# Identity products beside the waits of TensorE in a two-layer decoder kernel

## The chip, the cores and the metric

The kernel runs as one program on one core of a Trainium2 chip. The metric is the device time of one execution in microseconds (us), the median of several runs; lower is better.

## The reference, cut to what matters

```python
x = x + _L0_attn_ref(_layernorm(x), ...)                     # state-space scan, 8 x 512 x 256
x = x + _L0_xattn_ref(_layernorm(x), ctx_1024, ctx_1024, ...) # attention, 16 heads of 16, 1024 keys
x = x + _L0_ffn_ref(_layernorm(x), ...)                      # three quantised blocks with LoRA
x = x + _L1_attn_ref(_layernorm(x), ...)                     # self-attention, 16 heads of 16, 512 keys
x = x + _L1_xattn_ref(ctx_1024, _layernorm(x), ...)          # latent attention, 16 heads of 64, 1536 keys
x = x + _L1_ffn_ref(_layernorm(x), ...)                      # ternary weights, integer activations
...
attn = jax.nn.softmax(jnp.einsum('bhqd,bhkd->bhqk', q, k) * SCALE, axis=-1)
out = jnp.einsum('bhqk,bhkd->bhqd', attn, v)
```

The softmax of each attention is computed against the exact maximum of each row, so the kernel computes the scores twice: once for the maxima, and once more, shifted, for the exponentials.

## The kernel before

`build` runs one `phase` after another: constants, ssm_inputs, scan, ssm_outputs, attention_inputs (tiles `ci_`), attention (`ca_`, 1024 keys), lora_ffn (`ff_`), attention_inputs (`ai_`), attention (`aa_`, 512 keys), latent_inputs (`li_`), latent_attention (`la_`) and ternary_ffn (`tf_`). Each phase ends with a barrier of all engines (L3317), so that no engine begins the next before all have finished.

`attention` walks 32 units (8 sequences x 4 groups of 4 heads). A unit has KT key tiles, 8 in `ca` and 4 in `aa`; "a key tile" below is one turn of the loop `for kt in range(KT)`. In it TensorE issues, in this order written by hand, the scores of four heads (L1765, one 512-column product each, into three banks of PSUM that `ScalarE` must have emptied), the products of exponentials and values of the key tile before (`weigh`, L1774, eight records), and between them a part of the work of the next unit: the maximum pairs (`max_pair`, L1758). A pair is two products of 48 rows side by side in the array, and VectorE reduces its 1024 columns to row maxima (L1898). The two pair banks make a pair wait until the pair two before it is reduced. When the last pair of a unit is reduced, VectorE negates and transposes the maxima, and a DMA (`shift_row`, L1701) writes them as an extra row of the queries; the unit's scores wait for it (`shift_done`).

Before unit 0 there is an opening: 19 pairs in `ca` (`MP + FIRST`, MP = 16) and 11 in `aa` (MP = 8), then two products that make the bias (L1808), and then the wait for the shift row. Unit 0's key tiles carry further pairs to catch up (`CATCH_UP`): in `ca` 3, 3, 3, 2, 2 and so on, in `aa` 2, 3, 3, 3. The last pair of all belongs to unit 31. Behind it come key tiles without a pair: in `ca` the last three of unit 30 and the eight of unit 31, 11 in all; in `aa` the last two and the four, 6 in all. Then a tail: `turn`, `turn_back` and five `project` (L1798), each with a copy or sum on another engine.

`latent_inputs` ends with value projections and stores; SyncE must load `lw_nT` back before the barrier opens. `latent_attention` begins with three projections, 12 maximum pairs (`max_pair`, L2705), four transposes of the negated maxima (`shifts`, L2713), two copies by ScalarE (L2847), and then its units' scores (L2722, L2723). `ternary_ffn` begins with a normalisation on VectorE, GpSimd and ScalarE, after which TensorE turns the tokens (L3075).

Of the kernel before, what the change touches and what calls it, by code (L numbers as in the profile page):

```python
# [13 lines left out]
P = 128  # L14
B, T, D = 8, 512, 256
TC = 1024
NT = T // P
KD = D // P
# [45 lines left out]
def sems(nc, ctx, tag, names):  # L64

    made = [nc.alloc_semaphore(f"{tag}_{n}") for n in names.split()]
    ctx.extend(made)
    return made


class NormBuffers:
# [1533 lines left out]
def attention(nc, io, g, semctx, tag, keys, loads, bo, bv, beside=None):  # L1605
# [8 lines left out]
    MP = GH // 2 * NT * HALVES  # L1614
    assert MP == 2 * KT
    UNITS = B * GROUPS
# [2 lines left out]

    AHEAD, FIRST = 6, 3  # L1620
    OUT, TURN, BACK = 0, 2, 3
    PAIRS = {8: (2, 2, 2, 2, 2, 2, 2, 2), 4: (1, 3, 1, 3)}[KT]
    CATCH_UP = {8: (1, 1, 1, 0, 0, 0, 0, 0), 4: (1, 0, 2, 0)}[KT]
    assert sum(PAIRS) == MP and sum(CATCH_UP) == AHEAD - FIRST
# [47 lines left out]
    with ExitStack() as ctx:  # L1672
# [31 lines left out]
        with nc.Block() as block:  # L1704
# [21 lines left out]
            def _(pe):  # L1726
# [74 lines left out]

                for j in range(MP + FIRST):
                    max_pair(j)
                pe.wait_ge(w_loaded, 16)
                pe.wait_ge(bias_step, KD)
                out = max_banks("bias", 0)
                for k in range(KD):
                    last = pe.matmul(out[:, 0, 0:D], bv_wide[:, k, :], w_o[:, k, :], start=(k == 0), stop=(k == KD - 1))  # L1808
                last.then_inc(bias_step, 1)
                pe.wait_ge(ones_loaded, 32)  # L1810
                for unit in range(UNITS):
                    u = unit % GROUPS
                    pe.wait_ge(shift_done, 64 * (unit + 1))
                    for kt in range(KT):
                        early, late, behind = pairs_of(unit, kt)
                        scores(unit, u, kt, 0)
                        scores(unit, u, kt, 1)
                        for j in early:
                            max_pair(j)
                        for kind, n in after(unit, kt):  # L1820
                            if kind == "turn":
                                turn(n)
                            elif kind == "back":
                                turn_back(n)
                            else:
                                project(n)
                        scores(unit, u, kt, 2)
                        for j in late:
                            max_pair(j)
                        scores(unit, u, kt, 3)  # L1830
                        if kt > 0:
                            weigh(unit, u, kt - 1)
                        elif unit > 0:
                            weigh(unit - 1, (u - 1) % GROUPS, KT - 1)
                        for j in behind:
                            max_pair(j)
                weigh(UNITS - 1, GROUPS - 1, KT - 1)
                turn(UNITS - 1)
                turn_back(UNITS // 2 - 1)
# [602 lines left out]
def latent_inputs(nc, io, g, semctx, weights):  # L2442
# [3 lines left out]
    with ExitStack() as ctx:  # L2446
# [13 lines left out]
        with nc.Block() as block:  # L2460
# [18 lines left out]
            @block.tensor  # L2479
            def _(pe):  # L2480
                pe.wait_ge(xv_loaded, 16)
                for b in range(B):
                    values.project(pe, b, 0, xv)
                    values.project(pe, b, 1, xv)
                    pe.wait_ge(xnorm2.normed, NT * b + NT)

                    if b:
                        pe.wait_ge(nT_done, KD * b)
                    for c in range(KD):
                        for j in range(NT):  # L2490
                            last = pe.transpose(tp[:, c, j * P:(j + 1) * P], xn[:, j, c * P:(c + 1) * P], g.ident[:, :])
                    last.then_inc(lat_ready, 1)
                    values.project(pe, b, 2, xv)
                    values.project(pe, b, 3, xv)

            @block.scalar
            def _(act):
# [41 lines left out]
def latent_attention(nc, io, g, semctx, weights):  # L2539
# [19 lines left out]
    with ExitStack() as ctx:  # L2559
# [57 lines left out]
        with nc.Block() as block:  # L2617
# [45 lines left out]
            def _(pe):  # L2663
# [147 lines left out]
                pe.wait_ge(v_done, 1)  # L2811
                for n in range(NM):
                    max_pair(0, 0, 0, n)
                shifts(0)
                units(unit_steps)
                for x in range(2):
                    for h in range(2):
# [187 lines left out]
def ternary_ffn(nc, io, g, semctx):  # L3005

    KI = INNER // P
    with ExitStack() as ctx:
# [46 lines left out]
        with nc.Block() as block:  # L3055
# [12 lines left out]
            @block.tensor  # L3068
            def _(pe):
                def turn_tokens(b):  # L3070
                    pe.wait_ge(xq_done, b + 1)
                    pe.wait_ge(xT_done, b)
                    for c in range(KD):
                        for j in range(NT):
                            last = pe.transpose(tp[:, c, j * P:(j + 1) * P], xq[:, j, c * P:(c + 1) * P], g.ident_bf[:, :])  # L3075
                    last.then_inc(tp_ready, 1)

                def gate(n):
                    if n % NT == 0:
                        pe.wait_ge(xT_done, n // NT + 1)  # L3080
                    pe.wait_ge(gated_done, n)
                    hidden(n, g_ps, w_gate).then_inc(g_ready, 1)

                def up(n):
                    pe.wait_ge(h_done, n)
                    hidden(n, u_ps, w_up).then_inc(u_ready, 1)

                def hidden(n, ps, w):
                    rows = slice(n % NT * P, n % NT * P + P)
                    for half in range(2):  # L3090
                        for k in range(KD):
                            last = pe.matmul(ps[:, half, :], xqT[:, k, rows], w[:, k, half * T:(half + 1) * T],  # L3092
                                             start=(k == 0), stop=(k == KD - 1))
                    return last

                def turn_hidden(n):
                    pe.wait_ge(hq_done, n + 1)
                    pe.wait_ge(hT_done, n)
                    for k in range(KI):
                        last = pe.transpose(ht_ps[:, k, :], hq[:, n % 2, k * P:(k + 1) * P], g.ident_bf[:, :])  # L3100
                    last.then_inc(ht_ready, 1)

                def down(n):
                    pe.wait_ge(hT_done, n + 1)
                    pe.wait_ge(x_done, n)
                    for k in range(KI):
                        last = pe.matmul(y_ps[:, 0:D], hqT[:, k, :], w_down[:, k, :], start=(k == 0), stop=(k == KI - 1))  # L3107
                    last.then_inc(y_ready, 1)

                turn_tokens(0)  # L3110
                pe.wait_ge(w_loaded[0], 16)
                gate(0)
                pe.wait_ge(w_loaded[1], 16)
                up(0)
                for n in range(TILES + LAG):
                    if n >= LAG:
                        if n == LAG:
                            pe.wait_ge(w_loaded[2], 16)
                        down(n - LAG)
                    if n + 1 < TILES:  # L3120
                        gate(n + 1)
                        up(n + 1)
                    if 0 < n <= TILES:
                        turn_hidden(n - 1)
                    if of(n, INTEGERS) is not None:
                        turn_tokens(of(n, INTEGERS))
# [304 lines left out]
```

## Time and profile before

| | us |
|---|---|
| median of 3 runs | 5219.44 |
| lowest and highest | 5215.84, 5220.12 |
| the profiled execution: its time | 5224.77 |
| its span, first to last instruction | 5222.9 |
| TensorE busy | 4837.2 (93%) |
| VectorE busy | 3661.5 (70%) |
| ScalarE busy | 2929.2 (56%) |
| GpSimd busy | 2638.9 (51%) |
| mean granted TensorE clock | 0.965 |

The granted clock is given as a share of 2.4 GHz: 1.00 is 2.4 GHz and 0.50 is 1.2 GHz. A busy TensorE is not TensorE at its peak, since its matmuls are pipelined and their ends are modelled. Starts are microseconds from the start of the span.

### The profile page before, as it was taken

What the parts mean: (1) busy time and instruction counts of PE and PEld (TensorE: products, weight loads), DVE (VectorE), ACT (ScalarE), POOL (GpSimd) and SP (SyncE); (2) the same over time, 40 slices, a digit from 0 to 9 for tenths busy, and PEclk for the clock granted to TensorE, in tenths of its full rate; (3) what the DMA queues carried; (4) which work ended last, traced back from release to release, by engine and by line L of the source; (5) the groups of instructions that cost most, each with busy time, mean ns of one, the idle gap of its engine ahead of it and who ended that gap; (6) DMA issues with size and microseconds to landing.
All of it is one profiled execution on the core that took longest, in us unless ns stands there. A gap on an engine that the chain in (4) does not pass through costs nothing. (4 is left out here: it accounts for less than half of the span.)

```text
span 5222.9 us, 71135 instructions
## 1 busy us (share of the span) xinstructions
PE 4837.2 (93%) x23995; PEld 2650.3 (51%) x24010; DVE 3661.5 (70%) x6589; ACT 2929.2 (56%) x6224; POOL 2638.9 (51%) x1552
## 2 busy tenths in 40 slices
PE   6899997799999898899879999999999999999976
PEld 5555555344444487444455555555555555555533
DVE  8666666688888588688746666666666766666668
ACT  5677773377777543476534444444444444444557
POOL 5555554200000142521037777777777778787740
PEclk9999998799999799899989999999999999999989
DMA  6566667432222003523363433334333333333300
GB/s 220 192 232 240 230 235 224 132 84 74 72 74 69 12 1 113 178 85 87 114 195 75 100 85 90 91 83 97 80 94 85 89 97 81 94 89 85 89 17 29
DMA packets 344187, 576.29 MB, mean 110 GB/s; under 512 B 49120, under 2 KB 142368, under 8 KB 342800
## 3 DMA queue, kind: packets, MB, share of 16 engines
q1 hardware_dynamic: 341616, 567.53, 37.7%
q8 instruction: 193, 3.16, 0.2%
q10 hardware_dynamic: 2208, 4.20, 0.2%
q14 instruction: 170, 1.39, 0.1%
HBM read 335.54 MB, written 201.85 MB: 103 GB/s over the span
## 5 line engine op out<-in xcount | busy, mean ns | idle before, releaser
L2913 POOL TENSOR_TENSOR la_acc<-la_acc,la_pr 128x1024 f32<-128x1024 f32 x704 | 1697.0, 2411 | 494.5 <-ACT la_pr L2871 459.2
L2871 ACT ACTIVATE la_pr<-la_s_ps 128x512 f32<-128x512 f32 x1536 | 793.7, 603 | 973.2 <-PE la_s_ps L2723 971.5
L2730 PE MATMUL la_o_ps<-la_pr,la_vf 128*64 128x512 f32 x3072 | 743.8, 605 | 0.0
L2722 PE MATMUL la_s_ps<-la_q_hl,la_k_hh 128*128 128x512 f32 x1536 | 691.6, 450 | 1.8 <-ACT la_q_hs L2847 1.4
L1898 DVE TENSOR_REDUCE ca_mx<-ca_m_ps 128x2 f32<-128x1024 f32 x512 | 600.8, 1217 | 118.7 <-PE ca_m_ps L1758 118.5
L1860 ACT ACTIVATE ca_pr<-ca_s_ps 128x512 f32<-128x512 f32 x1024 | 542.1, 601 | 215.6 <-PE ca_s_ps L1765 212.3
L2940 DVE TENSOR_REDUCE la_mx<-la_m_ps 128x2 f32<-128x1024 f32 x384 | 462.9, 1206 | 215.3 <-PE la_m_ps L2705 206.7
L2723 PE MATMUL la_s_ps<-la_q_hs,la_k_l 65*128 65x512 f32 x1536 | 608.8, 396 | 0.0
L2940 DVE TENSOR_REDUCE la_mx<-la_misc 128x2 f32<-128x1024 f32 x384 | 466.1, 1214 | 0.0
L2722 PEld LDWEIGHTS la_s_ps<-la_q_hl,la_k_hh 128*128 128x128 f32 x1536 | 290.0, 189 | 243.4 <-ACT la_pr L2871 103.7
L2730 PEld LDWEIGHTS la_o_ps<-la_pr,la_vf 128*64 128x64 f32 x3072 | 186.3, 136 | 346.8 <-issue 227.3
L1898 DVE TENSOR_REDUCE aa_mx<-aa_m_ps 128x2 f32<-128x1024 f32 x256 | 306.2, 1216 | 66.5 <-PE aa_m_ps L1758 63.3
L1860 ACT ACTIVATE aa_pr<-aa_s_ps 128x512 f32<-128x512 f32 x512 | 275.5, 602 | 118.5 <-PE aa_s_ps L1765 118.3
L1765 PE MATMUL ca_s_ps<-cl_qs,cl_ks 49*128 49x512 f32 x1024 | 330.2, 474 | 8.8 <-ACT ca_pr L1860 5.5
L2723 PEld LDWEIGHTS la_s_ps<-la_q_hs,la_k_l 65*128 65x128 f32 x1536 | 292.3, 190 | 36.1
L2314 POOL MEMSET ff_bias<- 128x768 f32 x1 | 0.7, 737 | 611.7 <-POOLq L3317 611.7
L2952 DVE RECIPROCAL la_rden<-la_den 128x128 f32<-128x128 f32 x256 | 241.3, 944 | 88.4 <-ACT la_den L2857 88.4
L2964 DVE TENSOR_TENSOR g_x<-g_x,la_misc 128x512 f32<-128x512 f32 x128 | 88.0, 688 | 303.5 <-PE la_misc L2749 303.5
L1758 PE MATMUL ca_m_ps<-cl_ks,cl_qs 48*128 48x512 f32 x1024 | 254.8, 493 | 45.6 <-DVE ca_mx L1898 34.7
L1774 PE MATMUL ca_o_ps<-ca_pr,cl_vs 128*32 128x512 f32 x2048 | 283.8, 628 | 0.0
L1765 PEld LDWEIGHTS ca_s_ps<-cl_qs,cl_ks 49*128 49x128 f32 x1024 | 137.5, 193 | 240.0 <-ACT ca_pr L1860 188.7
L916 PE MATMUL sc_jobs<-sc_n_parts,cw_xk 128*128 128x512 f32 x768 | 246.7, 429 | 0.0
(405 smaller groups left out, 8822.8 us busy)
## 6 DMA issues: line engine op xcount, KB each, us to landing
la_k_hh<-scratch_k_high SPq DMA_DIRECT2D x128, 512.0 KB, 6.5
scratch_k_high<-sc_k_high SPq DMA_DIRECT2D x128, 256.0 KB, 2.6
scratch_k_low<-sc_k_low SPq DMA_DIRECT2D x128, 256.0 KB, 2.8
la_w_parts<-scratch_w_parts SPq DMA_DIRECT2D x64, 512.0 KB, 6.2
la_k_l<-scratch_k_low SPq DMA_DIRECT2D x64, 512.0 KB, 8.4
la_vf<-scratch_xv SPq DMA_DIRECT2D x64, 512.0 KB, 4.2
cl_ks<-scratch_k_rows SPq DMA_DIRECT2D x384, 64.0 KB, 2.8
scratch_vaug<-sc_v SPq DMA_DIRECT2D x16, 1024.0 KB, 4.4
```

What stands on the lines that cost most here:

```text
L916: return pe.matmul(jobs[:, bank, :], stationary, moving, start=(i == 0), stop=(i == len(products) - 1))
L1758: last = pe.matmul(out[:, i, :], qs[rows, u, r, qt:T:NT], ks[rows, u, r, half * T:(half + 1) * T], start=True, stop=True)
L1765: pe.matmul(out, ks[rows, u, r, kt * P:(kt + 1) * P], qs[rows, u, r, :], start=True, stop=True).then_inc(s_ready, 1)
L1774: last = pe.matmul(o_ps[32 * h:32 * h + 32, :], vs[:, u, kt, h, :], pr[:, 2 * (kt % 2) + h // 2, h % 2, :], start=(kt == 0), stop=(kt == K ...
L1860: act.activation(pr[:, 2 * (kt % 2) + h // 2, h % 2, :], s_ps[:, s_turns.bank("tile", n), :], ACT.Exp, scale=scale).then_inc(p_done, 1)
L1898: dve.tensor_reduce(mx[:, unit % 2, qt, r:GH:2, half], m_ps[:, m_turns.bank("max", j), :, :], AX.X, ALU.max).then_inc(m_reduced, 1)
L2722: pe.matmul(s_ps[:, bank, :], k_hh[:, par, h, keys], q_hl[:, par, h, :], start=True, stop=False)
L2723: pe.matmul(s_ps[:, bank, :], k_l1[:, par, h, keys], q_hs[:, par, h, :], start=False, stop=True).then_inc(s_ready, 1)
L2730: last = pe.matmul(o_ps[XD * h:XD * h + XD, :], vf[:, par, st, XD * h:XD * h + XD], pr[:, st % LAG, h, :], start=(st == 0), stop=(st == XT ...
L2871: act.activation(pr[:, st % LAG, h, :], s_ps[:, (2 * st + h) % 3, :], ACT.Exp, scale=scale).then_inc(p_done, 1)
L2913: pool.tensor_tensor(total, total, exps, ALU.add).then_inc(acc_done, 1)
L2940: dve.tensor_reduce(mx[:, qt, :, c], pair_banks(i)[:, :, :], AX.X, ALU.max).then_inc(m_reduced, 1)
```

## The change

A helper `keep_busy(pe, g, bank, count)` issues `count` products of the 128 x 128 f32 identity with itself, with no wait and no signal, into a part of a PSUM bank that nothing reads then. It is called:

- in `attention` (both), three products behind each of the opening pairs, 24 behind the bias products, and three at the end of each key tile that has no pair (with a wait that all pairs are reduced);
- at the end of `latent_inputs`, 36 products;
- in `latent_attention`, three behind each of the 12 opening pairs, and 16 behind the transposes of `shifts(0)`;
- at the start of `ternary_ffn`, 48 products ahead of `turn_tokens(0)`.

```diff
+def keep_busy(pe, g, bank, count):
+
+    for _ in range(count):
+        pe.matmul(bank, g.ident[:, :], g.ident[:, :], start=True, stop=True)
...
+    BESIDE_PAIR, BESIDE_SHIFT = 3, 24
...
                 for j in range(MP + FIRST):
                     max_pair(j)
+                    keep_busy(pe, g, o_ps[:, 0:P], BESIDE_PAIR)
                 pe.wait_ge(w_loaded, 16)
                 pe.wait_ge(bias_step, KD)
...
                 last.then_inc(bias_step, 1)
+                keep_busy(pe, g, o_ps[:, 0:P], BESIDE_SHIFT)
                 pe.wait_ge(ones_loaded, 32)
...
                         for j in behind:
                             max_pair(j)
+                        if not early + late + behind:
+                            pe.wait_ge(m_reduced, MP * UNITS)
+                            keep_busy(pe, g, m_ps[:, 0, 1, 0:P], BESIDE_PAIR)
...
                     values.project(pe, b, 3, xv)
+                pe.wait_ge(nT_done, KD * B)
+                keep_busy(pe, g, tp[:, 0, 0:P], 36)
...
                 for n in range(NM):
                     max_pair(0, 0, 0, n)
+                    keep_busy(pe, g, s_ps[:, 0, 0:P], 3)
                 shifts(0)
+                keep_busy(pe, g, s_ps[:, 2, 0:P], 16)
                 units(unit_steps)
...
+                keep_busy(pe, g, y_ps[:, D:D + P], 48)
                 turn_tokens(0)
```

## Rows read from the trace of the kernel before

**Rows 1.** Windows: length; busy (count) of PE, PEld, DVE, ACT, POOL; clock, DMA share, GB/s.

```profile
974.40:1022.20 47.80, 40.40 (x126) 16.85 (x127) 38.64 (x40) 12.55 (x22) 18.79 (x9) 0.50 0.10 29
...
1742.60:1762.60 20.00, 19.36 (x65) 5.74 (x65) 1.10 (x3) 10.38 (x20) 0.00 (x0) 0.50 0.00 0
1770.00:1790.00 20.00, 17.83 (x60) 7.75 (x60) 1.52 (x4) 6.29 (x12) 0.00 (x0) 0.50 0.00 1
...
2148.40:2162.20 13.80, 13.75 (x50) 6.33 (x49) 10.07 (x11) 6.87 (x14) 13.12 (x6) 0.50 0.51 139
2556.00:2572.00 16.00, 14.79 (x86) 5.53 (x84) 1.78 (x5) 13.27 (x26) 0.00 (x0) 1.00 0.01 2
...
2663.70:2668.70 5.00, 4.70 (x12) 3.42 (x12) 1.31 (x2) 1.38 (x3) 2.72 (x3) 0.63 1.04 237
5029.70:5040.20 10.50, 0.00 (x0) 0.00 (x0) 6.08 (x25) 4.15 (x8) 2.29 (x6) 0.50 0.42 150
```

**Rows 2.** Timeline: eight f32 products of 128 columns; start, length, what, idle before.

```profile
2670.68 3.60 PE L2675 MATMUL la_misc<-lw_w_v,lw_nT 128*128 128x128 f32 x16 [2.21 <-DVE la_k_l L2935]
...
2701.96 2.02 PE L2675 MATMUL la_misc<-lw_w_v,lw_nT 128*128 128x128 f32 x16 [2.26 <-DVE la_k_l L2935]
```

**Rows 3.** Timeline of VectorE and TensorE in the opening of `ca`.

```profile
975.37 18.20 DVE L1898 TENSOR_REDUCE ca_mx<-ca_m_ps 128x2 f32<-128x1024 f32 x16 [0.57 <-PE ca_m_ps L1758]
...
996.53 2.04 PE L1808 MATMUL ca_m_ps<-cl_w_o,ca_bv_wide 128*128 128x256 f32 x4 [0.41 <-DVE ca_mx L1898]
998.50 0.79 PE L1765 MATMUL ca_s_ps<-cl_qs,cl_ks 49*128 49x512 f32 x2
```

**Rows 4.** Timeline in unit 0 of `ca`: one key tile's pairs, two `weigh`.

```profile
1007.20 3.49 DVE L1898 TENSOR_REDUCE ca_mx<-ca_m_ps 128x2 f32<-128x1024 f32 x3 [1.69 <-PE ca_m_ps L1758]
...
1022.79 1.07 PE L1774 MATMUL ca_o_ps<-ca_pr,cl_vs 128*32 128x512 f32 x8
...
1025.46 1.07 PE L1774 MATMUL ca_o_ps<-ca_pr,cl_vs 128*32 128x512 f32 x8
```

**Rows 5.** Timeline behind the last pair of `ca`, and its last sum on VectorE.

```profile
1740.22 1.06 PE L1774 MATMUL ca_o_ps<-ca_pr,cl_vs 128*32 128x512 f32 x8
...
1764.63 1.07 PE L1774 MATMUL ca_o_ps<-ca_pr,cl_vs 128*32 128x512 f32 x8
...
1766.87 0.49 PE L1765 MATMUL ca_s_ps<-cl_qs,cl_ks 49*128 49x512 f32 x1 [0.51 <-ACT ca_pr L1860]
1767.29 1.07 PE L1774 MATMUL ca_o_ps<-ca_pr,cl_vs 128*32 128x512 f32 x8
...
1778.35 3.64 PE L1774 MATMUL ca_o_ps<-ca_pr,cl_vs 128*32 128x512 f32 x16
...
1792.37 0.42 DVE L1926 TENSOR_TENSOR g_x<-g_x,ca_m_ps 128x256 f32<-128x256 f32 x1 [0.44 <-PE ca_m_ps L1798]
```

**Rows 6.** Timeline of `aa`: bias, `weigh` in unit 0, last `weigh`, last sum.

```profile
2146.49 2.04 PE L1808 MATMUL aa_m_ps<-al_w_o,aa_bv_wide 128*128 128x256 f32 x4 [0.41 <-DVE aa_mx L1898]
...
2163.28 1.06 PE L1774 MATMUL aa_o_ps<-aa_pr,al_vs 128*32 128x512 f32 x8
...
2571.12 2.11 PE L1774 MATMUL aa_o_ps<-aa_pr,al_vs 128*32 128x512 f32 x16
...
2580.51 0.42 DVE L1926 TENSOR_TENSOR g_x<-g_x,aa_m_ps 128x256 f32<-128x256 f32 x1 [0.44 <-PE aa_m_ps L1798]
```

**Rows 7.** Timeline: last projection of `li`; `la`: GpSimd's first, first score, next projections.

```profile
2648.60 3.01 PE L1078 MATMUL li_cv_banks<-li_xv,li_cv_parts 128*128 128x512 f32 x12
...
2660.53 5.21 POOL L2897 MEMSET la_k_l<- 1x6144 f32 x1 [21.19 <-POOLq L3317]
...
2691.99 0.79 PE L2722 MATMUL la_s_ps<-la_q_hl,la_k_hh 128*128 128x512 f32 x1 [1.35 <-ACT la_q_hs L2847]
...
2695.57 4.13 PE L2668 MATMUL la_misc<-la_n_parts,la_w_parts 128*128 128x512 f32 x12
```

**Rows 8.** Timeline: the first work of TensorE in `tf`.

```profile
5040.26 1.03 PE L3075 MATMUL tf_tp<-g_ident_bf,tf_xq 128*128 128x128 bf16 x8 [12.40 <-DVE tf_xq L3228]
```

## The prediction

> **What bounds the kernel now.** I read the page first: TensorE is busy 93% of the span, and the row of the granted clock falls below full in a few of the 40 slices. Then windows, to find which stretches run at 1.2 GHz and what TensorE did in them; then the timeline of each of those, to see whether TensorE or another engine sets the pace there. Only where TensorE sets it is a higher clock worth anything.
>
> Two attention phases, one opening and one ending each, and two phase starts matter. In `ca` the clock is 0.50 through the opening and unit 0, although TensorE is busy 40.40 of 47.80 us, and again twice behind the last pair, with 19.36 of 20 us busy [rows 1]. In `aa` unit 0 is at 0.50 too, but the key tiles behind its last pair stay at 1.00 [rows 1]: that end has nothing to win. In the openings VectorE sets the pace, one reduction in 1.14 us (18.20 over 16) [rows 3]. Behind the last pair it is a loop: scores, an exponential, the last score (which waits 0.51 us for ScalarE), `weigh`, next scores; 2.66 us a key tile at full clock [rows 5].
>
> **The price of the filler.** The nearest rows are the value projections, eight f32 products of 128 columns in 16 records: 2.02 us at full clock, 3.60 us at half [rows 2]. Without the drain of the last that is 0.23 and 0.43 us a product. So three cost 0.7 (1.3), sixteen 3.7, 24 cost 5.5 (10.3), 36 cost 8.3 and 48 cost 11 us (numbers in brackets at half clock). A filler waits for nothing, but what stands behind it on TensorE waits for it. A bound below: if the identity product were one record, half of this.
>
> **Opening of `ca`.** The half clock at the start of `la` lasted 0.74 of 5.0 us, 3.7 us from the first dense products [rows 1]. That is the lower bound for the rise; the upper is that it does not rise, as in unit 0 of `ca`. I take 4 to 5 us, since the fillers, like that start, use the whole array. Until then a pair with its fillers costs 0.43 (512 columns at 1.2 GHz) + 1.3 = 1.7 us against VectorE's 1.14: three pairs, 1.7 us late. Afterwards 0.2 + 0.7 hides behind VectorE. The bias starts at 996.53 + 1.7 = 998.2, takes 1.0 instead of 2.04, and then stand 24 fillers: scores at 1004.7 instead of 998.50 [rows 3], 6.2 us late. The shift row gives them no cover, or little: it had landed by 998.50 [rows 3], and moves with the reductions to about 1000.2. Queued behind them are the first scores, and behind those ScalarE's exponentials and VectorE's next pairs. Unit 0 then runs at full clock, but its first three key tiles carry three pairs each, and VectorE needs 3.49 us for three [rows 4]; the next two cost 2.67 each, as from 1022.79 to 1025.46 [rows 4]. So `weigh` of the sixth key tile comes at 1004.7 + 3 x 3.5 + 2 x 2.67 + 1.4 = 1022.0 against 1022.79 [rows 4]. Gain 0.8; bounds, from the rise and the bank waits: gain 3 to loss 1.5.
>
> **End of `ca`.** From 1740.22 to 1778.35 there are ten key tiles in 38.1 us [rows 5]. The fillers stand behind `weigh` and ahead of the next scores, so they do not fill the 0.51 us in which TensorE waits; they lengthen the loop to 2.66 + 0.7 = 3.36 us. Ten at full clock with one projection (0.3) are 33.9: gain 4.2. The added wait for the last reduction costs nothing: VectorE had it well before the `weigh` of that key tile ended. The tail lasted 1778.35 to 1792.79, 14.4 us, in `ca` [rows 5], and at full clock 9.8 in `aa` (2571.12 to 2580.93) [rows 6]; with one more group of fillers 10.5. Gain 3.9. Together 8.1, bounds 4 (clock lost in the tail) to 9.
>
> What holds the clock there? `aa` held it through 16 us whose key tiles carry turns and projections, at 14.79 of 16 us busy, while `ca` lost it at 19.36 of 20 us busy [rows 1]. The longest wait in the loop is about 0.5 us. The Trainium skill, page "TensorE: Matmul & The Clock Gate", section "Loop structure matters more than you think", holds that matmuls issued back to back stay warm and that a long wait between them makes the engine cold. By that rule gaps of 0.5 us cost no clock, and fillers that leave these gaps where they are could not hold it either; the trace does not agree that gaps alone decide. I take the fillers, whole-array products like the turns of `aa`, to hold it.
>
> **Opening of `aa`.** By the same steps: bias at 2146.49 + 1.7 = 2148.2, scores at 2154.7. Unit 0 has 2, 3, 3 pairs: 2.67 + 3.5 + 3.5, with 0.3 for VectorE's negation and 1.4 to the `weigh`: 2166.1 against 2163.28 [rows 6]. Loss 2.8, bounds 1 to 4.5. Four key tiles are too few to win back 6 us where VectorE is nearly the bound.
>
> **End of `aa`.** Six groups of 0.7 in a loop already at full clock [rows 1]: loss 4.2, bounds 2.5 (some fall into waits) to 5.
>
> **`li` to `la`.** TensorE is done at 2651.6; 36 fillers end at 2659.9, and the next phase begins on GpSimd at 2660.53 [rows 7], a barrier of about 1 us included: loss 0.3, bounds 0 to 1.3. The clock gains nothing, since TensorE then idles some 4 us for its weights. In the opening of `la` three fillers hide behind each reduction: loss 0.3. The sixteen behind the shift transposes take 3.7 us where TensorE waited 1.35 [rows 7]; less 0.5 for faster transposes, the scores start 1.85 late. Then eight score products and twelve projections, 3.6 + 4.13 us mostly at half clock [rows 7], become about 4.8: gain 2.9. Sum of `la`: gain 0.7, bounds gain 3.5 to loss 2.
>
> **Start of `tf`.** TensorE is idle and at 0.50 from 5029.7 to 5040.2 [rows 1]. The 48 fillers start at half clock: 4.5 us for ten, then 38 x 0.23 = 8.7, end 5043.1, 2.9 us after the tokens are ready [rows 8]. Behind them wait the turn, the gate and up products. At full clock the turn (1.03) and eight products of 512 columns save 1.7. Loss 1.2, bounds gain 1 to loss 3.
>
> **Sum.** -0.8 - 8.1 + 2.8 + 4.2 + 0.3 - 0.7 + 1.2 = -1.1 us. Against the profiled execution's 5224.8 that is 5223.7. The median of the runs, 5219.4, lies 5.3 lower, so I forecast 5218.3. All gains at their bounds together give 5204, all losses 5234 (2 us either way for the clock in `ff`, whose start moves).
>
> **Rivals.** 0.2% is 10.4 us, about what a measurement can tell from no change.
> - *The fillers do not hold the clock behind the last pair of `ca`* (slower). Speaks for it: `ca` lost its clock at 97% busy. Against: `aa`. Then some seven key tiles at half clock pay 1.3 each and the others 0.7, 12.1 in all, instead of a gain of 8.1: 5238. It decides from the point at which about half of those tiles are cold. This is the time that the page's rule on gaps, named above, would give as well.
> - *The clock does not rise in the openings at all.* 18 and 10 pairs 0.6 late, 24 fillers at 10.3: some 21 us in `ca` and 16 in `aa`: 5254. Against it: the start of `la` rose within 3.7 us [rows 1].
> - *The filler costs half* (faster). If the identity product is one record, as the transposes with the identity are, the shift fillers give back 5.5, the end of `ca` 3.8, that of `aa` 2.1, `la` 1.9, `tf` 2.9, `li` 0.3: 5202. Against it: the f32 products of the same shape are two records each [rows 2].
> - *The fillers change nothing*, all hidden: excluded, since 24 products cost at least 2.8 us.
>
> The Trainium skill, same page, section "Back-to-back issue gap", gives about 81 ns a product of 128 columns in a stream with weight loads; by it 24 would cost 1.9 us and the sum would be about -21, an estimate of 5198. The rows show 0.23 us for f32.
>
> **How the numbers follow.** Forecast 0.70 (of it 0.05 beyond 0.2% on the fast side and 0.03 on the slow one), clock lost behind the last pair 0.13, no rise 0.05, half price 0.12. Faster 0.17, same 0.62, slower 0.21. The likeliest case's own range is 5207 to 5230; the range given, 5204 to 5238, reaches to the first rival and nearly to the third and leaves out the second.
>
> **What would show it.** In the profile after: the clock at 1.00 from about 5 us into each opening; the first score of `ca` some 6 us later after its opening than before; unit 0 bound by VectorE; key tiles of 3.36 us behind the last pair in both attentions; TensorE's tokens in `tf` turned about 3 us after they are ready. Wrong would be the forecast if a group of three fillers took under 0.5 us, if the clock fell behind the last pair of `ca`, or if the clock in `lora_ffn`, untouched by the edit, came out otherwise by more than some 2 us.

## The result, and the profile after

The changed kernel takes 5252.99 us (median of 4 runs, 5249.33 to 5255.73) against 5219.78 of the kernel before beside it. The ratio is 1.0055, 95% interval 1.0039 to 1.0071: slower by 29 us (20 to 37); the two medians lie 33 us apart. The forecast was 5218.3, with 5238 as its upper end. The profiled execution took 5252.26 us, its span is 5250.5, and its mean granted clock is 0.975, higher than the 0.965 of before. So the mean clock is higher, and the time longer. Two runs among those below, one of end_only at 5366.98 us and one of the kernel before at 8590.73, are in a slower state and are left out of the changes in per cent.

Windows of the changed kernel (columns as in [rows 1]): the opening of `ca` up to the rise of the clock, its rest, and the 24 products; behind the last pair of `ca`; the opening of `aa`; its first unit; behind its last pair; the start of `tf`.

```profile
974.00:981.00 7.00, 6.96 (x26) 5.03 (x26) 4.04 (x5) 0.00 (x0) 0.20 (x1) 0.51 0.01 2
981.00:1003.60 22.60, 22.60 (x129) 16.86 (x129) 19.36 (x18) 0.99 (x1) 0.00 (x0) 1.00 0.02 5
1003.60:1010.00 6.40, 6.40 (x56) 6.18 (x54) 0.99 (x2) 0.29 (x1) 4.83 (x3) 1.00 0.57 151
...
1742.80:1762.80 20.00, 17.91 (x108) 8.06 (x106) 3.34 (x5) 12.84 (x25) 0.00 (x0) 1.00 0.01 1
...
2132.80:2158.20 25.40, 25.39 (x89) 18.36 (x90) 14.40 (x15) 1.28 (x1) 0.17 (x1) 0.50 0.10 27
...
2164.70:2180.00 15.30, 14.35 (x69) 6.61 (x68) 12.95 (x13) 9.19 (x18) 13.88 (x7) 0.89 0.33 108
2566.00:2586.00 20.00, 19.02 (x118) 9.07 (x114) 3.81 (x9) 13.76 (x27) 0.00 (x0) 1.00 0.01 1
...
5055.20:5067.80 12.60, 12.53 (x98) 12.55 (x99) 6.08 (x25) 4.15 (x8) 3.75 (x9) 0.86 0.34 126
```

The clock column has 1.00 where [rows 1] had 0.50, after 7.0 us in `ca` and, in this execution, only behind the 25.4 us of pairs in `aa`. Beside it stands the price: in the openings TensorE has no idle time left, and VectorE, which set the pace before, is busy 14.40 of 25.40 us in `aa`.

The opening of `ca` on TensorE. The pairs are now L1765, the identity products L74, the bias L1816, the scores L1772:

```profile
974.04 0.81 PE L1765 MATMUL ca_m_ps<-cl_ks,cl_qs 48*128 48x512 f32 x2 [10.82 <-PEq L3334]
974.78 1.65 PE L74 MATMUL ca_o_ps<-g_ident 128*128 128x128 f32 x6
976.36 0.81 PE L1765 MATMUL ca_m_ps<-cl_ks,cl_qs 48*128 48x512 f32 x2
...
980.98 0.62 PE L1765 MATMUL ca_m_ps<-cl_ks,cl_qs 48*128 48x512 f32 x2
981.53 0.94 PE L74 MATMUL ca_o_ps<-g_ident 128*128 128x128 f32 x6
982.40 0.62 PE L1765 MATMUL ca_m_ps<-cl_ks,cl_qs 48*128 48x512 f32 x2
...
1003.60 1.03 PE L1816 MATMUL ca_m_ps<-cl_w_o,ca_bv_wide 128*128 128x256 f32 x4
1004.47 5.52 PE L74 MATMUL ca_o_ps<-g_ident 128*128 128x128 f32 x48
1009.92 0.51 PE L1772 MATMUL ca_s_ps<-cl_qs,cl_ks 49*128 49x512 f32 x2
```

and on VectorE (L1910 was L1898):

```profile
983.06 1.23 DVE L1910 TENSOR_REDUCE ca_mx<-ca_m_ps 128x2 f32<-128x1024 f32 x1 [0.18 <-PE ca_m_ps L1765]
...
1010.70 5.75 DVE L1910 TENSOR_REDUCE ca_mx<-ca_m_ps 128x2 f32<-128x1024 f32 x5 [5.61 <-PE ca_m_ps L1765]
```

At half clock a pair follows the pair before by 976.36 - 974.04 = 2.32 us, at full clock by 982.40 - 980.98 = 1.42, and VectorE, which reduces one in 1.14 [rows 3], now waits for TensorE at each. Of the 1.42 the pair takes 0.55 and the three products 0.87. While the 24 run, VectorE idles 5.61 us.

The weight load of a pair, on its own row, lasts 0.31 us:

```profile
982.40 0.31 PEld L1765 LDWEIGHTS ca_m_ps<-cl_ks,cl_qs 48*128 48x128 f32 x2
```

The columns of the pair take 0.21 us at full clock and 0.43 at half, an estimate from 512 columns; the pair takes 0.55 and 0.74, some 0.3 more in both cases. A weight load that nothing hides would account for it, and so might the change between row pairs and the whole array. No run tells the two apart, so the cause is open.

Behind the last pair of `ca`, one key tile:

```profile
1746.33 1.06 PE L1781 MATMUL ca_o_ps<-ca_pr,cl_vs 128*32 128x512 f32 x8
1747.33 0.94 PE L74 MATMUL ca_m_ps<-g_ident 128*128 128x128 f32 x6
1748.19 0.73 PE L1772 MATMUL ca_s_ps<-cl_qs,cl_ks 49*128 49x512 f32 x3
1749.43 0.50 PE L1772 MATMUL ca_s_ps<-cl_qs,cl_ks 49*128 49x512 f32 x1 [0.51 <-ACT ca_pr L1872]
1749.86 1.07 PE L1781 MATMUL ca_o_ps<-ca_pr,cl_vs 128*32 128x512 f32 x8
```

A key tile lasts 1749.86 - 1746.33 = 3.53 us, and the wait of 0.51 us for ScalarE is still there [rows 5]: the products stand outside it.

The table is made from the starts of the same instructions in three profiles of the kernel before and two of the changed one (the further ones are among the experiments), in us. The forecasts are the terms of the sum; that of an opening is compared with first to last pair, in which the first unit's gain is contained.

| stage | before | after | change of the means | forecast |
|---|---|---|---|---|
| start to first pair of `ca` | 974.4, 974.6, 975.0 | 974.0, 977.4 | +1.0 | 0 |
| `ca`, first pair to last pair | 762.3, 762.1, 762.2 | 768.8, 768.7 | +6.5 | -0.8 |
| last pair of `ca` to start of `ff` | 57.0, 49.3, 49.4 | 50.6, 50.6 | -1.3 | -8.1 |
| `ff` and `ai`, to first pair of `aa` | 339.8, 344.7, 341.4 | 339.4, 339.7 | -2.4 | 0 |
| `aa`, first pair to last pair | 419.5, 418.9, 422.0 | 433.6, 426.6 | +10.0 | +2.8 |
| last pair of `aa` to start of `li` | 29.0, 29.0, 28.9 | 34.0, 34.1 | +5.1 | +4.2 |
| `li` | 78.5, 82.7, 81.0 | 83.8, 81.6 | +2.0 | +0.3 |
| `la`, start to first score | 31.5, 31.2, 31.8 | 34.8, 36.7 | +4.3 | -0.7, with the next row |
| `la`, first score to start of `tf` | 2337.8, 2338.4, 2333.8 | 2336.3, 2332.8 | -2.1 | |
| `tf`, start to first turn | 10.5, 10.5, 10.4 | 12.4, 12.4 | +1.9 | +1.2 |
| rest of `tf` | 182.6, 185.1, 185.0 | 182.8, 182.8 | -1.4 | 0 |
| span | 5222.9, 5226.5, 5220.9 | 5250.5, 5243.4 | +23.5 | -1.1 |

The two rows from first to last pair carry 16.5 of the 23.5 us. (The rounded rows add up to 23.6.)

### The profile page after: what moved, and what is told of

It reads as the page before. It is cut to its first block and busy times, and to the rows that moved or that the text cites. A ratio compares the mean times of both kernels' runs of the same rounds, so it can differ in the third digit from the quotient of the medians.

```text
span 5250.5 us, 72435 instructions
## 1 busy us (share of the span) xinstructions
PE 4897.7 (93%) x24645; PEld 2729.5 (52%) x24660; DVE 3663.8 (70%) x6589; ACT 2928.8 (56%) x6224; POOL 2638.7 (50%) x1552
## 5 line engine op out<-in xcount | busy, mean ns | idle before, releaser
L1910 DVE TENSOR_REDUCE ca_mx<-ca_m_ps 128x2 f32<-128x1024 f32 x512 | 602.1, 1217 | 124.6 <-PE ca_m_ps L1765 124.6
L1910 DVE TENSOR_REDUCE aa_mx<-aa_m_ps 128x2 f32<-128x1024 f32 x256 | 306.7, 1216 | 79.8 <-PE aa_m_ps L1765 76.6
L1772 PE MATMUL ca_s_ps<-cl_qs,cl_ks 49*128 49x512 f32 x1024 | 322.0, 461 | 9.6 <-ACT ca_pr L1872 6.2
L1765 PE MATMUL ca_m_ps<-cl_ks,cl_qs 48*128 48x512 f32 x1024 | 249.0, 483 | 40.4 <-DVE ca_mx L1910 29.6
L1772 PEld LDWEIGHTS ca_s_ps<-cl_qs,cl_ks 49*128 49x128 f32 x1024 | 134.3, 188 | 224.4 <-ACT ca_pr L1872 185.0
```

The costliest lines, as they stand in the source:

```text
L1765: last = pe.matmul(out[:, i, :], qs[rows, u, r, qt:T:NT], ks[rows, u, r, half * T:(half + 1) * T], start=True, stop=True)
L1772: pe.matmul(out, ks[rows, u, r, kt * P:(kt + 1) * P], qs[rows, u, r, :], start=True, stop=True).then_inc(s_ready, 1)
L1910: dve.tensor_reduce(mx[:, unit % 2, qt, r:GH:2, half], m_ps[:, m_turns.bank("max", j), :, :], AX.X, ALU.max).then_inc(m_reduced, 1)
```

## The experiments

All are edits of the changed kernel; products that are not named are left out. Changes in per cent are against runs of the kernel before on the same chip. 0.1% is 5.2 us. The kernels ran on three chips: open_only, end_only, later_only and pairs_no_shift on number 12, before_again, fewer_beside, end_wait and bf16_beside on 10, and the other four on 3. So medians of different chips are not to be compared with each other (the kernel before had 5221.68, 5222.39 and 5217.5 us there).

### One group of places at a time

```diff
-    BESIDE_PAIR, BESIDE_SHIFT = 3, 24
+    BESIDE_PAIR, BESIDE_SHIFT, BESIDE_END = {open_only: (3, 24, 0), end_only: (0, 0, 3),
+        later_only: (0, 0, 0), pairs_no_shift: (3, 0, 0), shift_only: (0, 24, 0)}
...
-                            keep_busy(pe, g, m_ps[:, 0, 1, 0:P], BESIDE_PAIR)
+                            keep_busy(pe, g, m_ps[:, 0, 1, 0:P], BESIDE_END)
```

The diff is condensed: it shows the numbers of the five kernels in one line. `later_only` keeps the products of `li`, `la` and `tf`, which the four others leave out.

**open_only.** 

> Only the fillers of the two attention openings: three beside each pair and 24 behind the bias. Theory A, the openings carry the loss: the trace of the changed kernel has ca's last pair 6.5 us later after ca's first pair than before, and aa's 14.1; nothing else moves, so 5219.8 + 20.6 = 5240. Theory B, the terms of the prediction were right there (-0.8 and +2.8) and the loss lies elsewhere, as in a changed clock of the later phases: 5222.

**end_only.** 

> Only the three fillers in each key tile without a pair, in ca and aa. Theory A: from the last pair to the next phase ca takes 6.4 us less (57.0 to 50.6) and aa 5.0 more (29.0 to 34.0), since ca keeps its clock and both pay 0.86 us a group: 5218.4. Rival: the clock in ca was held by the fillers of the opening only through a shift of phase in time, and it falls again: then both pay, some 12 and 5 us: 5237.

**later_only.** 

> Only the fillers at the end of latent_inputs, in the opening of latent_attention and ahead of ternary_ffn. In the trace of the changed kernel the phase li took 5.3 us more, la 1.8 and tf 2.1. Theory A: li's 5.3 are not from the fillers, whose products end 2.5 us before the next phase begins, but from transfers and clock falls inside the phase that came out otherwise; then li costs 0 to 0.5 here and the sum is 5224. Rival: the fillers delay li's end: 5229.

**pairs_no_shift.** 

> Three fillers beside each opening pair of ca and aa, none behind the bias. Theory A: at full clock a pair and its fillers take 1.42 us (2.32 at half), more than the reduction's 1.14, so the pairs alone make ca's bias 7 us and aa's 12 us late; without the 24 the scores start 5.5 us sooner than in open_only, but half of that is lost again where the clock is not up. 5230 to 5236. Theory B, the 24 carry the loss and the pairs are hidden: 5222.

**shift_only.** 

> The 24 products behind the bias in ca and aa alone; no products beside pairs, none elsewhere. Theory A (what the openings lose is TensorE's time that nothing hides, the 24 as well as the threes): the bias starts where it does in the kernel before, 22.1 us behind the first pair in ca and 13.0 in aa; the 24 take 8 to 10.3 us, since they start at half clock; the first scores come 8 to 10 us later than in the kernel before; unit 0 at full clock gives back about 4 us of it in ca and 2 in aa; time 10 to 14 us above before (0.2 to 0.3%). With the 12.4 of the threes alone that adds up to the 25 of both. Rival B (the 24 are nearly free once nothing stands beside the pairs, because a warm unit 0 wins it back): time within 4 us of before, and the loss of the two together comes from the threes.

| kernel | median us | change, 95% interval | first to last pair, `ca` and `aa` |
|---|---|---|---|
| open_only | 5246.88 | +0.47% (0.31 to 0.63) | 779.5, 432.9 |
| pairs_no_shift | 5234.63 | +0.22% (0.13 to 0.31) | 765.3, 424.7 |
| shift_only | 5235.67 | +0.27% (0.16 to 0.38) | 768.9, 430.2 |
| end_only | 5229.3 | +0.11% (0.01 to 0.22) | 762.5, 421.7 |
| later_only | 5220.86 | +0.08% (-0.08 to 0.23) | 762.3, 424.5 |

Openings, ends and later places add up to 0.66%, against 0.55% (0.39 to 0.71) for all; within the openings the threes and the 24 add up to 0.49% against 0.47%. So the loss is mainly the openings', and both kinds of products have their share. Of later_only the interval holds zero.

The last column is of one profile each, and those executions are not always typical: they took 5249.15 us in open_only, 5225.68 in pairs_no_shift (9.0 under its median), 5244.24 in shift_only (8.6 over), 5233.33 in end_only and 5236.84 in later_only (16.0 over). The runs of open_only fall into two near 5234 us at a mean clock of 0.971 and four from 5245 to 5256 at 0.965 to 0.967; the profile is of the second kind.

Against what was expected: open_only bears out theory A, somewhat above its 5240. pairs_no_shift is in theory A's range; its bias came 7.4 us late in `ca`, as expected, but 4.3 and not 12 in `aa`, where the clock was up sooner. end_only missed both times, 5218.4 and 5237: the clock held and `aa` paid 5.1 us, as theory A has it, but `ca` did not win 6.4 us over the typical execution of before, as shown further down. later_only does not tell its theories apart.

What the clock did in them, in windows. First open_only, the opening of `ca` up to the rise, and that of `aa`:

```profile
976.50:1011.00 34.50, 34.50 (x120) 24.81 (x120) 18.68 (x17) 0.00 (x0) 0.15 (x1) 0.50 0.00 1
...
2138.50:2154.50 16.00, 15.97 (x56) 11.60 (x56) 8.90 (x9) 0.00 (x0) 0.20 (x1) 0.50 0.03 13
```

TensorE is busy in 34.50 of 34.50 us and stays at 0.50. The same instructions had the clock up after 7 us in both profiles of the changed kernel and in pairs_no_shift, which ran on the same chip as open_only. In `aa` the clock rose after 16 us here, after 26 and 11.6 in the two profiles of the changed kernel and after 5 in pairs_no_shift. In later_only, in the opening of `la`, it did not rise during the pairs:

```profile
2671.90:2699.90 28.00, 27.96 (x98) 19.95 (x99) 14.88 (x13) 0.00 (x0) 0.00 (x0) 0.50 0.43 101
```

and the first score came 46.2 us behind the phase's start, against 31.2 to 31.8 before. When the clock rises is thus not fixed by the code. By the rule of the Trainium skill that the prediction weighed (page "TensorE: Matmul & The Clock Gate", section "Loop structure matters more than you think"), products issued back to back stay warm; here they stood back to back for 34.5 us and the engine remained at 1.2 GHz. The engine was cold at the start, so this does not refute that warm products stay warm, but it shows that density alone did not warm it.

Then shift_only: bias and the 24 of `ca`, and the first unit behind them:

```profile
998.40:1007.30 8.90, 8.88 (x54) 8.42 (x54) 1.43 (x2) 1.05 (x1) 6.30 (x3) 0.71 0.52 148
1010.70:1031.20 20.50, 20.40 (x78) 7.95 (x79) 13.87 (x14) 9.43 (x19) 8.87 (x4) 0.51 0.00 1
```

While the 24 run the clock rises, and it falls again 3 us behind them, for 20 us. The first score came 31.0 us after the first pair against 24.1 before, and the last pair 6.7 us late: 0.2 us of the delay was given back in `ca`, and 10.1 us were lost in `aa`. Theory A is right about the loss and wrong about the 4 and 2 us given back; its 8 to 10 us for the delay of the first scores were 6.9 and 7.1.

### Fewer products beside a pair

```diff
-    BESIDE_PAIR, BESIDE_SHIFT = 3, 24
+    BESIDE_PAIR, BESIDE_SHIFT, BESIDE_END = {'ca': (1, 0, 0), 'aa': (2, 0, 0)}[tag]
```

**fewer_beside.** 

> One product beside each opening pair of ca and two beside each of aa; no 24, nothing at the end, in li, la or tf. Theory A (a pair takes about 0.56 us of TensorE and each identity product 0.23 us at full clock, with 0.1 to 0.2 once for the group; 0.74 and 0.43 at half clock; this and not VectorE sets the pace in the changed kernel): with one product 0.9 to 1.0 us at full clock and 1.3 at half, so VectorE's 1.14 sets the pace in ca at full clock; with two 1.15 to 1.25 at full clock and 1.7 to 1.9 at half in aa. Rival B (the price is one of changing between row pairs and whole-array products, once for each group, whatever its size): the cadence stays near 1.4 us at full clock and 2.3 at half with one product and with two. If A, the clock should rise late or not at all with one product, since TensorE does less than with three.

A single execution, in which the products of `li`, `la` and `tf` are left out as well: 5224.53 us, span 5222.7. One product in `ca`, then two in `aa`:

```profile
976.07 0.81 PE L1765 MATMUL ca_m_ps<-cl_ks,cl_qs 48*128 48x512 f32 x2
976.81 0.79 PE L74 MATMUL ca_o_ps<-g_ident 128*128 128x128 f32 x2
977.54 0.81 PE L1765 MATMUL ca_m_ps<-cl_ks,cl_qs 48*128 48x512 f32 x2
...
2119.38 0.81 PE L1765 MATMUL aa_m_ps<-al_ks,al_qs 48*128 48x512 f32 x2
2120.13 1.22 PE L74 MATMUL aa_o_ps<-g_ident 128*128 128x128 f32 x4
2121.28 0.81 PE L1765 MATMUL aa_m_ps<-al_ks,al_qs 48*128 48x512 f32 x2
```

From pair to pair 1.47 us with one, 1.90 with two, 2.32 with three, all at half clock: 0.43 for each product, as forecast from [rows 2], on a base of 1.04. Rival B, a price for the change to the whole array whatever its size, falls as the main cost; but the base is there. The forecast had counted 0.43 us of columns for the pair and nothing else, so 0.6 us of each turn was missing from it. Some 0.3 of this is in the pair (0.74 for 0.43), as above; the other 0.3 lies in the group of products (1.58 us for three, where three times 0.43 are 1.29), and its cause is open. With only one product the turn at half clock (1.47, expected 1.3) is already longer than VectorE's 1.14, and the clock stayed at half through both openings; the turns at full clock that theory A gave were thus not seen. First to last pair took 764.8 us in `ca` and 431.3 in `aa`.

### The end of `ca`: several profiles of one kernel, and where the products stand

**before_again.** 

> The kernel before, unchanged, profiled once more. Theory A (its clock held behind the last pair of ca in three of three kernels without fillers there, so that the fall in the first profile belongs to that execution): last pair of ca to the start of lora_ffn 42.7 us, the clock at 1.00. Rival B (fillers in other phases kept the clock up in those three): 57 us again, as in the first profile, with the clock at 0.50 from about 1742 us.

**before_third.** 

> The kernel before, profiled a third time. Of three executions of the same code up to lora_ffn the clock fell behind the last pair of ca in two (57.0 and 49.3 us to lora_ffn) and held in one (42.7). Theory A (a fall there is a matter of the execution): one of the three figures or one between, most likely 42.7 to 50. Rival B (the kernel before always falls there, and another kernel's later phases hold it by chance): 49 to 57.

Both are the kernel before, unchanged: 5228.26 and 5222.75 us. The changed kernel was profiled again too (after_again, 5245.16 us, beside these on record). For it theory A was that the rise of the clock is a matter of the execution, with 30 to 47 us from first pair to first score in `ca` and 25 to 32 in `aa`; rival B, that the code fixes it, with 35.9 and 31.9 again within 1. It had 35.8 and 26.3: the second figure speaks against B. Windows behind the last pair, of before_again:

```profile
1738.00:1748.00 10.00, 8.65 (x40) 2.30 (x36) 1.63 (x3) 6.78 (x14) 0.00 (x0) 0.73 0.01 2
1748.00:1758.00 10.00, 9.68 (x36) 2.94 (x28) 0.42 (x1) 4.85 (x9) 0.00 (x0) 0.50 0.00 0
```

and of later_only, whose instructions are the same up to `li`, with its one short fall, and the whole stretch of fewer_beside:

```profile
1738.00:1748.00 10.00, 8.42 (x49) 2.42 (x47) 2.72 (x4) 7.84 (x16) 0.00 (x0) 1.00 0.01 2
1748.00:1758.00 10.00, 8.96 (x52) 3.49 (x54) 1.10 (x3) 8.23 (x17) 0.00 (x0) 1.00 0.00 1
...
1767.90:1771.30 3.40, 3.40 (x17) 0.80 (x17) 0.00 (x0) 1.34 (x3) 0.00 (x0) 0.51 0.00 0
...
1737.90:1779.10 41.20, 33.65 (x188) 13.01 (x186) 6.80 (x14) 26.31 (x51) 0.00 (x0) 1.00 0.00 1
```

From the last pair of `ca` to the start of `ff`, without products there: 57.0, 49.3 and 49.4 us in the kernel before, 57.0 in shift_only, where the clock fell for some 20 us once or twice; 42.7 in open_only, pairs_no_shift and later_only, where it fell for 3.4 us only; and 41.3 in fewer_beside, where it did not fall. With three products behind the weighing: 50.6, 50.6 and 50.7 (end_only), at 1.00. The clock did not fall at all in any of the six profiles, of five kernels, with products there (the three kernels below included), and in one of eight without, so that the products very likely hold it. But as written they cost 8.0 us where it nearly holds by itself, and gain 6.4 only over the worst case. Neither theory on the kernel before is settled: all three of its profiles had a long fall (before_again missed both expected figures, and before_third fits both theories), while four of the five other kernels without products there had none. The chip is a rival that no run excludes: the chip of the first profile is not on record; of the others without products, the three on chip 12 had no long fall, the two on chip 3 did, and of the two on chip 10 one did. With products the clock held on all three chips.

```diff
                         scores(unit, u, kt, 2)
+                        if BESIDE_END and not early + late + behind:
+                            pe.wait_ge(m_reduced, MP * UNITS)
+                            keep_busy(pe, g, m_ps[:, 0, 1, 0:P], BESIDE_END)
```

**end_wait.** 

> Two identity products in each of the 11 key tiles of ca without a pair, placed where TensorE waits 0.51 us for ScalarE (behind the third score product, ahead of the last) and not behind the weighing; nothing else of the change. Theory A (the loss at this end is 0.86 us of TensorE's own time a key tile because the fillers stand outside the wait): a key tile takes 2.7 to 2.8 us, last pair to lora_ffn 43 to 44.5 us against 42.7 without and 50.7 with three behind the weighing; time within 0.1% of before. Rival B (any change to whole-array products costs the same wherever it stands): 3.2 to 3.5 us a key tile, 49 to 51 us for the stretch, and a time 6 to 8 us above before.

The whole edit is that call, with two products, in `ca` alone: 5217.13 us, -0.11% (-0.20 to -0.02).

```profile
1742.66 0.73 PE L1772 MATMUL ca_s_ps<-cl_qs,cl_ks 49*128 49x512 f32 x3
1743.32 0.71 PE L74 MATMUL ca_m_ps<-g_ident 128*128 128x128 f32 x4
1743.96 0.49 PE L1772 MATMUL ca_s_ps<-cl_qs,cl_ks 49*128 49x512 f32 x1
1744.38 1.06 PE L1781 MATMUL ca_o_ps<-ca_pr,cl_vs 128*32 128x512 f32 x8
...
1747.10 1.06 PE L1781 MATMUL ca_o_ps<-ca_pr,cl_vs 128*32 128x512 f32 x8
```

The wait for ScalarE is gone and the products stand in its place: 2.72 us a key tile against 2.66 without and 3.53 behind the weighing; the stretch takes 43.5 us at full clock. Theory A holds, rival B falls. The 43.5 are still 2.2 more than in fewer_beside: two of the key tiles carry a projection or a turn and had no such wait, and there the two products cost 1.06 us (3.98 against 2.92 in fewer_beside) and 0.80 (3.50 against 2.70). The mean of the eight profiles without products there is 47.8, so a gain of some 4 us is what the profiles lead one to expect of it.

### The identity in bf16

```diff
-        pe.matmul(bank, g.ident[:, :], g.ident[:, :], start=True, stop=True)
+        pe.matmul(bank, g.ident_bf[:, :], g.ident_bf[:, :], start=True, stop=True)
```

Six beside each opening pair of `ca`, `aa` and `la`, six inside the wait at both ends, none elsewhere.

**bf16_beside.** 

> The identity in bf16 instead of f32: six products beside each opening pair of ca, aa and la, six inside the 0.51 us wait of each key tile without a pair in ca and aa; no 24, 36, 16 or 48. Theory A (a bf16 product of 128 columns takes about 0.06 us at full clock and 0.12 at half, an estimate from the eight bf16 transposes of tf in 1.03 and 0.62 us): six take 0.4 to 0.5 us at full clock and 0.75 to 0.9 at half, the opening cadence is VectorE's 1.14 us at full clock and 1.5 to 1.7 at half, the ends cost nothing. If the clock rises within 10 us the openings lose 2 to 4 us in waiting and win it back in unit 0: time within 0.1% of before, 15 to 30 us under the changed kernel. Rival B (the clock does not rise under such a mixture): first pair to first score 30 us in ca and 19 in aa, and a time 8 to 14 us above before.

5224.67 us, +0.06% (-0.03 to 0.15). At the end of `ca` at full clock:

```profile
1747.55 0.51 PE L74 MATMUL ca_m_ps<-g_ident_bf 128*128 128x128 bf16 x6
1747.99 0.50 PE L1772 MATMUL ca_s_ps<-cl_qs,cl_ks 49*128 49x512 f32 x1
```

Six take 0.44 us, 73 ns each, against 0.23 us for the f32 product. The Trainium skill's figure for products of 128 columns in a stream (page "TensorE: Matmul & The Clock Gate", section "Back-to-back issue gap"), about 81 ns, is near this row and far from the f32 one. Behind the pairs the turn was 1.50 us, in the expected 1.5 to 1.7; the clock rose only 30 us into `ca`, and the first score came after 30.0 and 18.4 us, as rival B said. Yet first to last pair is 761.8 in `ca` and 426.4 in `aa`, and the time is that of before within the interval, which theory A gave for a clock that rises within 10 us, and rival B's loss of 8 to 14 us did not come. The ends were not free: in `aa` the stretch behind the last pair took 31.5 us against 29.0, and four of its key tiles grew by 0.4 to 0.9 us. Cheap products lose little and win nothing here.

### Products only where TensorE idles

```diff
                         project(b, K, k_ps, k_ready, k_low)
                         values(b)
+                keep_busy(pe, g, tp[:, 0, 0:P], 58 if own_keys else 24)
```

That is at the end of both input phases; with it the two products inside the wait of end_wait; nothing else.

**ahead_and_wait.** 

> Two identity products inside the 0.51 us wait of the 11 key tiles of ca without a pair, as before; and products in the idle time at the end of the two input phases (24 in front of ca, where TensorE idles 10.8 us; 58 in front of aa, where it idles 16), none beside the pairs. Theory A (only what TensorE does in an idle stretch is free; the clock follows what the engine last did): the first pair starts no later, the first pairs run at full clock, 0.6 us each instead of 0.8, unit 0 wins 2 to 6 us in ca and aa together; time 6 to 12 us under before. Rival B (the clock falls again in the opening, where a pair fills only half of VectorE's 1.14 us): first pair to last pair 762 us in ca and 420 in aa as before, and the time equals that of two products in the waits alone, about 5 us under before. Rival C (the products run on past the barrier): first pairs 2 to 10 us late, time above before.

5209.48 us, -0.17% (-0.28 to -0.05): faster than the kernel before, and than the changed one by some 0.7%. End of `ci` and start of `ca`:

```profile
967.17 5.52 PE L74 MATMUL ci_tp<-g_ident 128*128 128x128 f32 x48
979.45 1.24 PE L1766 MATMUL ca_m_ps<-cl_ks,cl_qs 48*128 48x512 f32 x4 [6.76 <-PEq L3330]
```

```profile
979.40:1001.40 22.00, 15.09 (x38) 5.85 (x38) 21.31 (x23) 0.10 (x1) 0.21 (x1) 0.50 0.00 1
```

The products end 6.8 us before the barrier opens, so TensorE delays nothing by them. The first pair is still the latest of the fourteen profiles (979.45, the others 973.1 to 977.4), but TensorE's own last product of `ci` ended 3.7 us later than in the first profile of before, ahead of the fillers. The clock is back at 0.50 when the pairs run. In this profile it rose 26 us into `ca` and stayed up but for 3.4 us, and first to last pair took 757.4 us against 762.2; in `aa` it rose after 38 us, later than the 28 to 29 of the kernel before, and the stretch took 425.0 us against 418.9 to 422.0. So the time is in the range of theory A, but its step, pairs at full clock, did not happen. The profiled execution took 5218.89 us, 9.4 more than the kernel's median, so it does not show what made the median fast. Whether the 4.8 us in `ca` are the products' doing one profile does not show; the intervals of end_wait and this kernel overlap, so the gain beyond the wait's is open.

## Why the prediction was wrong

**The step that failed** is, in the opening of `ca`: "Afterwards 0.2 + 0.7 hides behind VectorE", and with it the 1.7 us for a pair at half clock. The 0.7 for three products was nearly right (0.87 with what surrounds them), the 0.2 for the pair was its columns alone: in the row of starts it takes 0.55. The sum is 1.42 against VectorE's 1.14, so nothing hides at full clock either. Sixteen turns at 0.28 more and three at 1.18 more are 8.0 us; the bias came 29.6 us behind the first pair against 22.1, 7.5 later, where 1.7 was forecast. The first score was 11.8 us later relative to the first pair, forecast 6.2. Of the 24.7 us between the sum, -1.1, and the stages' +23.6 the two openings account for 14.5, the end of `ca` for 6.8 and `la` for 2.9; the other rows nearly cancel.

**The rise of the clock.** "I take 4 to 5 us" was measured as 7.0 in `ca`, twice, and as 26 and 11.6 in `aa`, where the forecast used the same figure. In the first of these two, with 11 turns at 2.32 us, the last pair of `aa` came 13.5 us late, in the second 6.5: +10.0 in the mean where +2.8 stood. The figure itself rested on one short stretch at the start of `la`. The same trace of before shows the clock at half again through the pairs of `la`:

```profile
2677.70:2698.20 20.50, 14.48 (x37) 8.18 (x38) 11.67 (x12) 3.56 (x6) 3.28 (x2) 0.50 0.50 110
```

A rise there did not last, and this the forecast did not weigh. The upper bound named, no rise at all, happened in open_only for the pairs of `ca` and in later_only in `la`; I had left it to a rival at 5 in 100.

**The 24.** Their price was right, 5.52 us forecast as 5.5, and so was what queues behind them. That unit 0 gives more back than was lost, 7.0 us for a delay of 6.2, did not happen: in the first profile of the changed kernel the first score was 11.8 us late and the last pair 6.5, so 5.3 came back; in shift_only, where the clock fell again, it was 0.2.

**End of `ca`.** The clock held under the fillers, as forecast, and the key tile is 3.53 us where 3.36 stood. Against the profiled execution of before the stretch gained 6.4 of the 8.1. But the term was taken from an execution that lost more than the others did (57.0 against 49.3 and 49.4, and 41.3 to 42.7 in four of five kernels with the same instructions there; from the last weighing on it took 15.4 us, in the two others of before 10.7). The step that was weak is "there are ten key tiles in 38.1 us", read as the kernel's state and not as one execution's.

**End of `aa`** was right in mechanism: +5.1, forecast 4.2, the difference being 0.86 a group for 0.7. **`tf`:** +1.9 for 1.2, within its bounds. **`li`:** first read as +5.3 us; end_only, with none of its products, shows 83.6, and seven other kernels without them 79.6 to 81.8, with 78.5 to 82.7 for the kernel before itself: so the difference lies within what executions differ by. **`la`:** +4.3 to the first score, and 2.1 less by the start of `tf`, which is inside the spread of the kernel before, where a gain of 0.7 stood. "In the opening of `la` three fillers hide behind each reduction" failed as it did in `ca`: a turn of the opening takes 1.30 us at full clock and 2.30 at half, both over the 1.2 of a reduction.

**The rivals.** The one at 5254, "the clock does not rise in the openings at all", comes within 1.0 us of the time, but it is not what happened in the profiled execution: there the clock was up for 22.6 of the 29.6 us in `ca`. That its number is near is luck: it charged the two openings with 37 us, they cost 16.5, and the end of `ca`, `la` and the spread of executions made up the difference. The clock behind the last pair of `ca` was not lost, and the product costs what the f32 rows said.

## What to carry to other kernels

Filler for the clock is nearly free inside a wait that TensorE has anyway, and costs its full time elsewhere: two products inside a wait of 0.51 us cost 0.06 us a turn, in the turns without that wait about 1, and three just outside it 0.87. Before giving an engine more work beside another that sets the pace, take its time for the present work from the distance of starts in a dense stretch and not from its columns; here 0.24 us of forecast room a turn was a deficit of 0.28. And how long the clock falls differs between executions of one kernel (57.0, 49.3 and 49.4 us for the same stretch), so take a second profile before pricing the remedy.

## What the runs showed of the hardware

- Identical instructions see different clocks: the opening of `ca` with three products a pair was at full clock after 7.0 us in three profiles and after 34.5 in a fourth; the end of `ca` without products had one or two falls of about 20 us in four profiles, one of 3.4 us in three and none in one.
- TensorE stayed at 1.2 GHz through 34.50 us of 34.50 busy, under pairs and whole-array products in turn; under the 48 whole-array products at the start of `tf`, with 1.88 us of idle time before them, the mean clock was 0.86 over 12.60 us.
- A pair of 48-row products between whole-array products takes 0.55 us at full clock and 0.74 at half, where its columns alone are 0.21 and 0.43; a whole-array f32 product of 128 columns 0.23 and 0.43, in bf16 0.07 at full clock.
- A higher mean clock (0.975 against 0.965) went with a longer time: the clock alone is no measure of such a change.
